# Second routing with per-batch inverses, scaling on the vector engine, normalisation on the scalar engine; feed-forward accumulators in two pairs of banks

## The reference

```python
x = x + 0.5 * ffn(layernorm(x))
x = x + attention(layernorm(x))
x = x + 0.5 * ffn(layernorm(x))
```

```python
att = softmax(where(causal, (q @ k.T) / sqrt(16), -1e10))
y = (att @ v).reshape(B, T, C) @ Wp.T + bp
```

## Time and profile before

| | us |
|---|---|
| median of 3 runs | 2720.24 |
| profiled execution, own time | 2707.74 |
| its span | 2706.0 |
| first feed-forward, about | 146 to 575 |
| attention, about | 575 to 2012 |
| second routing | 2012 to 2276 |
| second feed-forward | 2276 to 2706 |

### The profile page before, as it was taken

One profiled execution on the slowest core, in us unless ns is written; L12 is line 12 of the kernel. 1 busy time (PEld: TensorE's weight loads), 2 busy tenths in 40 slices (PEclk: granted clock), 3 DMA queues, 4 the chain that ended last, 5 costly groups with the idle time before them and its releaser, 6 DMA issues. The chain is left out here.

```text
span 2706.0 us, 43185 instructions
## 1 busy us (share of the span) xinstructions
PE 2227.9 (82%) x14740; PEld 1451.9 (54%) x14740; DVE 1699.0 (63%) x5181; ACT 1218.6 (45%) x2442; POOL 966.9 (36%) x1344
## 2 busy tenths in 40 slices
PE   6659999935699999999999999999962664899997
PEld 6658888834334444444444444443322664788886
DVE  7435555433477877877878878877733663555552
ACT  1224444411056665665666665666750212344443
POOL 3723434326423333333333333330002564333442
PEclk9999999965589999999999999999986775999999
DMA  9552223021524434435344344344315424323220
GB/s 341 187 197 96 88 71 104 29 73 58 132 64 110 117 84 111 112 86 130 87 110 114 86 97 111 80 105 99 80 60 124 144 69 165 126 71 100 77 71 22
DMA packets 185131, 283.21 MB, mean 105 GB/s; under 512 B 14392, under 2 KB 147704, under 8 KB 176720
## 3 DMA queue, kind: packets, MB, share of 16 engines
q1 hardware_dynamic: 170576, 247.08, 34.0%
q0 software_dynamic: 14336, 33.38, 3.5%
HBM read 153.99 MB, written 126.88 MB: 104 GB/s over the span
## 5 line engine op out<-in xcount | busy, mean ns | idle before, releaser
L1646 ACT ACTIVATE at_probs<-at_score_ps 128x512 f32<-128x512 f32 (+3 forms) x1536 | 692.9, 497 | 451.6 <-PE at_score_ps L1763 312.6
L1525 DVE CUSTOM_DVE_ANT_0 at_junk<-at_max_ps,at_causal 128x128 f32<-128x128 f32 (+3 forms) x1024 | 485.5, 484 | 128.2 <-PE at_max_ps L1749 126.2
L1749 PE MATMUL at_max_ps<-at_k,at_q 96*128 96x512 bf16 (+3 forms) x1536 | 494.1, 341 | 43.1 <-DVE at_peak L1525 30.7
L1760 PE MATMUL at_score_ps<-at_q,at_k 99*128 99x512 bf16 (+3 forms) x1536 | 499.3, 332 | 10.7 <-DMA at_v<-v_rows 4.4
L1528 DVE TENSOR_REDUCE at_peak<-at_max_ps 128x1 f32<-128x512 f32 x512 | 352.4, 688 | 118.2 <-PE at_max_ps L1749 114.9
L1037 DVE TENSOR_TENSOR f_hid_lo<-f_hid,f_hid_hi 128x512 fp32r<-128x512 f32 x256 | 177.5, 693 | 322.8 <-ACT f_hid_hi L1061 322.2
L1749 PEld LDWEIGHTS at_max_ps<-at_k,at_q 96*128 96x128 bf16 x1536 | 144.6, 98 | 398.0 <-DVE at_peak L1525 192.0
L1058 ACT ACTIVATE f_hid<-f_hid_ps 128x512 f32<-128x512 f32 x256 | 153.3, 599 | 413.7 <-PE f_hid_ps L1084 413.5
L1773 PE MATMUL at_o_ps<-at_probs,at_v 128*32 128x512 f32 (+3 forms) x3072 | 337.8, 512 | 1.2 <-ACT at_probs L1646 0.7
L1099 PE MATMUL f_y_ps<-f_w_hi,f_hid_hi 128*128 128x256 f32 x1024 | 292.7, 286 | 47.4 <-DVE f_xe L1015 28.9
L1099 PE MATMUL f_y_ps<-f_w_hi,f_hid_lo 128*128 128x256 f32 x1024 | 291.4, 285 | 0.0
(11 more groups left out here) (175 smaller groups left out, 3631.0 us busy)
## 6 DMA issues: line engine op xcount, KB each, us to landing
f_w_raw<-in_w SPq DMA_DIRECT2D x32, 1024.0 KB, 7.6
qk<-at_parts SPq DMA_DIRECT2D x32, 768.0 KB, 4.2
expert_in<-r_zeros SPq DMA_DIRECT2D x16, 1040.0 KB, 11.3
f_xe<-expert_in SPq DMA_DIRECT2D x32, 520.0 KB, 7.3
v_rows<-at_v_outs SPq DMA_DIRECT2D x32, 512.0 KB, 6.2
at_v<-v_rows SPq DMA_DIRECT2D x32, 512.0 KB, 10.4
o_rows<-at_o_out SPq DMA_DIRECT2D x64, 256.0 KB, 2.0
at_q<-qk SPq DMA_DIRECT2D x32, 384.0 KB, 7.6
```

The source lines that it names most:

```text
L1525: v.tensor_tensor_reduce(junk[bank(k, r)][:, 0:w], src, causal[:, HALF - w:HALF], 1.0, LEAST, ALU.add, ALU.max, out).then_inc(max_used, 1)
L1646: a.activation(probs[t % 2][:, h, c0:c0 + w], score_ps[(GH * t + h) % BANKS][:, 0:w], ACT.Exp, scale=float(SCALE)).then_inc(exp_done, 1)
L1749: te.matmul(max_ps[bank(u, r)][:, 0:w], q[u][0:ROWS, h, i * P:(i + 1) * P], kk[u][0:ROWS, h, k0:k0 + w], start=True, stop=True).then_inc(m ...
L1760: last = te.matmul(out[:, 0:w], kk[u][:, h, j * P:(j + 1) * P], q[u][:, h, hf * HALF + c0:hf * HALF + c0 + w], start=True, stop=not diagonal)
```

## The change

- The inverses of a batch are made in attention, while the next batch is at work: at the second group of batch b+1 SP loads the sums of batch b (128 x 128 values), DVE inverts them in the third group, and SP stores them in the fourth. Only the last batch's are made in the second routing, where they are needed for its own last batch only.
- In the second routing `scale` moves from POOL to DVE, at the head of DVE's loop; `normalize` moves from DVE to ACT, as an Identity with a scale of rstd and a bias of -mean x rstd (`shift`, one more small operation on POOL, one on DVE).
- The loads of outputs and inverses of batch 0 are issued first.
- In the feed-forwards the four accumulators lie by twos in a bank, and there are two such sets, used in turn by blocks; the first down of block b waits for combine(b-2) in place of combine(b-1).

```diff
@@ -486,6 +486,17 @@
+def sums_of(dr, b):
...
+    return (dr["o"].rearrange("(n v) t -> n v t", v=VW)[b * H:(b + 1) * H, D, :]
+            .rearrange("n (e t) -> n e t", t=H * S // P))
...
+def inverses_of(dr, b):
...
+    return dr["inv_sums"][b * H:(b + 1) * H, :].rearrange("n (e t) -> (n e) t", t=H * S // P)
...
 def second_route_block(nc, sh, dr, w):
@@ -513,12 +524,13 @@
         half = [sb(f"half{k}", [P, TPB], F32) for k in range(2)]
+        less_mean = [sb(f"less_mean{k}", [P, TPB], F32) for k in range(2)]
+        shift = [sb(f"shift{k}", [P, TPB], F32) for k in range(2)]
         bits = sb("bits", [P, TPB], I32)
...
         xn = sb("xn", [P, 2, TPQ, C], F32)
-        sums = xn[:].rearrange("p a j c -> p (a j c)")
-        assert TOK * H == P * 2 * TPQ * C
+        sums = sb("sums", [P, H * S // P], F32)
         xt = [sb(f"xt{k}", [P, TPQ, CC, P], F32) for k in range(2)]
@@ -585,34 +597,30 @@
-            sp.dma_start(sums, dr["o"].rearrange("(n v) t -> n v t", v=VW)[:, D, :]).then_inc(sums_loaded, 16)
+            load_o(0)
+            load_inverses(0)
             sp.dma_start(wp[:], dr["wp_t"].rearrange("(c p) o -> p c o", p=P)).then_inc(wp_loaded, 16)
-            load_o(0)
+            sp.dma_start(sums[:], sums_of(dr, B - 1)).then_inc(sums_loaded, 16)
             load_o(1)
+            load_inverses(1)
             sp.wait_ge(sums_inverted, 1)
-            sp.dma_start(dr["inv_sums"], sums).then_inc(sums_stored, 16)
-            sp.wait_ge(sums_stored, 16)
-            load_inverses(0)
-            load_inverses(1)
+            sp.dma_start(inverses_of(dr, B - 1), sums[:]).then_inc(sums_stored, 16)
             for b in range(2, B):
...
                 load_o(b)
+                if b == B - 1:
+                    sp.wait_ge(sums_stored, 16)
                 load_inverses(b)
...
         def _(pool):
-            def scale(b):
-                k = b % 2
-                pool.wait_ge(o_loaded[k], 16 * CC * (b // 2 + 1))
-                pool.wait_ge(inv_loaded, 16 * CC * (b + 1))
-                nc.gpsimd.tensor_tensor(o_in[k][:], o_in[k][:], o_inv[:], ALU.mult).then_inc(y_scaled, 1)
...
             def invert_std(b):
...
                 newton(nc.gpsimd, rstd[k][:].bitcast(F32), half[k][:], tmp[:], newton_step, NEWTON_STEPS * b, sh.passed)
+                nc.gpsimd.tensor_tensor(shift[k][:], less_mean[k][:], rstd[k][:].bitcast(F32), ALU.mult)
                 nc.gpsimd.tensor_copy(sh.x[:, TPB * b:TPB * (b + 1), RSTD], rstd[k][:].bitcast(F32)
@@ -625,15 +633,10 @@
-            scale(0)
-            scale(1)
             invert_std(0)
-            scale(2)
             for b in range(B):
...
                     invert_std(b + 1)
-                if b + 3 < B:
-                    scale(b + 3)
                 if b >= 1:
@@ -722,11 +725,28 @@
+            def normalize(n):
+                b, q = n // QPB, n % QPB
+                if b >= B:
+                    return
+                k = b % 2
+                if q == 0:
+                    act.wait_ge(rstd_ready, b + 1)
+                if n >= 2:
+                    act.wait_ge(xt_ps_ready, n - 1)
+                for a in range(TPQ):
+                    j = TPQ * q + a
+                    last = nc.scalar.activation(xn[:, q % 2, a, :], tile_of(sh.x, TPB * b + j), ACT.Identity,
+                                                bias=shift[k][:, j:j + 1], scale=rstd[k][:, j:j + 1].bitcast(F32))
+                last.then_inc(xn_ready, 1)
...
             act.wait_ge(wp_loaded, 16)
...
                     high(b, h)
+            normalize(0)
+            normalize(1)
             for b in range(B):
@@ -734,6 +754,7 @@
                     nc.scalar.copy(xt[q % 2][:], xt_ps[q % 2][:]).then_inc(xt_ready, 1)
+                    normalize(n + 2)
                     if q == 1 and b >= 1:
@@ -757,6 +778,12 @@
             per_expert = sh.expert_less[:].unsqueeze(1).to_broadcast([P, TPB, E])
...
+            def scale(b):
+                k = b % 2
+                dve.wait_ge(o_loaded[k], 16 * CC * (b // 2 + 1))
+                dve.wait_ge(inv_loaded, 16 * CC * (b + 1))
+                v.tensor_tensor(o_in[k][:], o_in[k][:], o_inv[:], ALU.mult).then_inc(y_scaled, 1)
@@ -779,20 +806,9 @@
                 dve.wait_ge(step, at + 2)
+                v.tensor_scalar(less_mean[k][:], moments[k][:, :, 0], -1.0, None, ALU.mult)
                 rsqrt_seed(v, moments[k][:, :, 1], half[k][:], bits[:], rstd[k][:], step, at + 2).then_inc(stats_ready, 1)
                 v.tensor_copy(sh.x[:, TPB * b:TPB * (b + 1), MEAN], moments[k][:, :, 0])
...
-            def normalize(b, q):
-                k, n = b % 2, QPB * b + q
-                if q == 0:
-                    dve.wait_ge(rstd_ready, b + 1)
-                if n >= 2:
-                    dve.wait_ge(xt_ps_ready, n - 1)
-                for a in range(TPQ):
-                    j = TPQ * q + a
-                    last = v.tensor_scalar(xn[:, q % 2, a, :], tile_of(sh.x, TPB * b + j), moments[k][:, j, 0:1],
-                                           rstd[k][:, j:j + 1].bitcast(F32), ALU.subtract, ALU.mult)
-                last.then_inc(xn_ready, 1)
@@ -834,37 +850,40 @@
                 v.memset(onehot[k][:], 0.0)
-            dve.wait_ge(sums_loaded, 16)
-            v.reciprocal(sums, sums).then_inc(sums_inverted, 1)
+            scale(0)
             dve.wait_ge(wp_hi_ready, 1)
...
                 low(0, h)
+            dve.wait_ge(sums_loaded, 16)
+            v.reciprocal(sums[:], sums[:]).then_inc(sums_inverted, 1)
+            scale(1)
             for b in range(2):
...
                     add(b, q)
+                    if b == 1 and q == 0:
+                        scale(2)
                     if q % 2:
...
             for b in range(B):
-                ahead = b + 2 < B
-                normalize(b, 0)
-                normalize(b, 1)
+                if b + 3 < B:
+                    scale(b + 3)
                 if b >= 1:
                     choose(b - 1)
-                for q in range(2):
-                    normalize(b, 2 + q)
-                    if ahead:
-                        add(b + 2, q)
+                if b + 2 < B:
+                    add(b + 2, 0)
+                    add(b + 2, 1)
                 if b + 3 < B:
...
                     place_rows(b - 1)
-                if ahead:
-                    for q in range(2, QPB):
-                        add(b + 2, q)
-                    if b + 3 < B:
-                        low(b + 3, 1)
+                if b + 2 < B:
+                    add(b + 2, 2)
+                    add(b + 2, 3)
+                if b + 3 < B:
+                    low(b + 3, 1)
+                if b + 2 < B:
                     measure(b + 2)
@@ -906,7 +925,7 @@
         hid_ps = [ps(f"hid_ps{k}", [P, BLK]) for k in range(2)]
-        y_ps = [ps(f"y_ps{k}", [P, C]) for k in range(TPK)]
+        y_ps = [[ps(f"y_ps{k}_{a}", [P, 2, C]) for a in range(TPK // 2)] for k in range(2)]
         xt_ps = [ps(f"xt_ps{k}", [P, BLK]) for k in range(CC)]
@@ -1012,7 +1031,7 @@
                 for t in range(TPK):
-                    last = v.scalar_tensor_tensor(x[:, t, 0:C], y_ps[t][:], x[:, t, COEF:COEF + 1], x[:, t, 0:C],
+                    last = v.scalar_tensor_tensor(x[:, t, 0:C], y_ps[b % 2][t // 2][:, t % 2, :], x[:, t, COEF:COEF + 1], x[:, t, 0:C],
                                                   ALU.mult, ALU.add)
@@ -1090,14 +1109,15 @@
                 pe.wait_ge(hid_lo_ready, FC * b + f + 1)
-                if f == 0 and b >= 1:
-                    pe.wait_ge(y_ready, b)
+                if f == 0 and b >= 2:
+                    pe.wait_ge(y_ready, b - 1)
                 m = f % NHID
...
                     for i, (a, w) in enumerate(((hid_hi, w2_hi), (hid_hi, w2_lo), (hid_lo, w2_hi))):
-                        last = nc.tensor.matmul(y_ps[t][:], a[m][:, rows], w[ws][:, f, :],
-                                                start=(f == 0 and i == 0), stop=(f == FC - 1 and i == 2))
+                        last = nc.tensor.matmul(y_ps[b % 2][t // 2][:, t % 2, :], a[m][:, rows], w[ws][:, f, :],
+                                                start=(f == 0 and i == 0 and t % 2 == 0),
+                                                stop=(f == FC - 1 and i == 2), skip_group_check=True)
                 last.then_inc(hid_free, 1)
@@ -1218,6 +1239,9 @@
         o_stored = [sem(f"o_stored{k}") for k in range(2)]
+        sums_loaded = sem("sums_loaded")
+        sums_inverted = sem("sums_inverted")
+        sums_stored = sem("sums_stored")
         block = ctx.enter_context(nc.Block())
@@ -1329,6 +1353,15 @@
                 store_o(g, 0)
+                done = g // NG - 1
+                if done >= 0 and g % NG == 1:
+                    for half in range(2):
+                        sp.wait_ge(o_stored[half], 16 * NG * (done + 1))
+                    sp.wait_ge(sums_stored, 16 * done)
```

(8 more changed lines are left out.)

## The result

The median is now 2643.49 us (2637.23 to 2645.89, 4 runs) beside 2719.99 for the kernel before (now 4 runs): a ratio of 0.9717, 95% interval 0.9699 to 0.9736, or 76.5 us less. The profiled execution took 2642.3 us, span 2640.5, which is 65.4 less than the profiled one of before (2707.74). The two differences are told apart by the blocks, read from where SP issues the first load of each.

What follows compares the result with a forecast made beforehand. PE was taken to bound feed-forwards and attention, a closed chain through POOL's queue the second routing (transfers after the change). -35.1 + 3 - 35.8 = -68 us, from the median 2720.2 to 2652 us, range 2634 to 2674.

Steps and rivals of the forecast that it cites:

- Feed-forwards, -35.1: Both feed-forwards: the block-start stall of 1.17 us goes in full, 15 x 2 times, 35.1 us less.
- rival (2): Feed-forwards: the stall only moves, to the low part or the shared bank; 10 of 35 us left, 2677; chance 0.06.
- rival (4): Feed-forwards: PE without its pauses loses its granted clock, slower than before, 2800 in its example; chance 0.03.
- Attention, +3: Attention: seven reciprocals on DVE ahead of the ring of maxima cost 3 us, the middle between 0 and 6.
- the upper bound: Attention: all DVE time of the seven reciprocals is passed on, 7 x 0.85 = 6 us.
- Start, 13 us earlier: Second routing, start: the first scale begins at 2031.4, 13 us before its row of 2044.5.
- Loop, bound by transfers at 17.8 us a batch: Second routing, loop: two pairs of loads a batch, 8.9 us each, take more time than any engine.
- The sum of the routing, -35.8: Second routing: its end comes at 2232.9 in place of 2268.7, 35.8 us less.
- The rule on 8 and 16 engines: Second routing loads: 8 heads in the slowest dimension limit them to 8 transfer engines; otherwise gain some 14 us larger.
- (1): Second routing: DVE's scales and lows hold up POOL, 4.7 us a turn; 20 us of gain gone, 2672; chance 0.13.
- (3): Second routing: transfers are not the bound, as loads of two kinds overlap better; 2638; chance 0.08.
- The sum on the median: Whole kernel: -68 us taken from the median of the runs, 2720.2, giving 2652 us.

Runs made afterwards that it cites:

- e1: The kernel before with only the feed-forward part of the change (two accumulator sets, wait for the combine two blocks back): 2682.15 us, ratio 0.9874.
- e2: The changed kernel with the old wait for the previous block's combine put back, accumulators still by twos in a bank: 2673.57 us, ratio 0.9843.
- e8: The changed kernel with five reciprocals in place of one at each of the seven places in attention: 2677.12 us, ratio 0.9854.
- e9: The changed kernel with scale back on POOL and normalisation back on DVE, leaving only the early start in the routing: 2670.79 us, ratio 0.9822.
- e4: The changed kernel with loads of outputs and inverses laid out with 16 rows outermost in place of 8 heads: 2631.33 us, ratio 0.9682.
- e3: The changed kernel with high put ahead of the normalisation on ACT in the second routing: 2627.05 us, ratio 0.9672.
- e7: The changed kernel with scale back on POOL, normalisation still on ACT: 2660.52 us, ratio 0.979.

## Why the prediction was right, and where it wasn't

- **Feed-forwards, -35.1.** Right in mechanism and size: 18.0 and 18.4 in the profiles, 35.7 in e1; pitch 23.50 as derived from the slices. PE idle alone (29.0) would have been too little; the pitch was the right measure. Sharing a bank costs 0 (e2), and PE keeps its clock, 1.00 in the second feed-forward: no rival (2), no rival (4).
- **Attention, +3.** One reciprocal measured 0.95 us, not 0.82, and costs nothing to be seen: attention was 1422.5 to 1431.8 us in the ten kernels with one, 1430.0 and 1435.5 in the two without. The middle between two bounds was taken where the slack of the ring was to be asked for; and the upper bound was none, as e8 shows: of each 4.9 us some 2.6 were covered, and what stuck out cost more than its own length.
- **Start, 13 us earlier.** The first scale is 15.6 us after the block's start, for 19.2 forecast and 32.3 before: the step holds, 3.6 too long since outputs and inverses together load faster than each alone. The block as a whole gained 9.1 us by the early start alone (e9).
- **Loop, bound by transfers at 17.8 us a batch: wrong.** This step failed. Its 8.9 us for a pair came from bytes over time in a stretch that the closed chain over POOL set. So it was what the chain asked for and not what the queues can give. At 205 GB/s a pair takes 1.05 / 0.205 = 5.1 us, 10.2 a batch, and e4 shows the late turns untouched by the rate. In place of it stood a chain that the forecast didn't look for. It costed ACT by its busy time ("no limit") and did not name what is queued on ACT behind the new wait for rstd, which was `high`. e3 shows this chain and its price, 15.3 us.
- **The sum of the routing, -35.8 for 39.3, is partly luck.** First to last scale took 119.2 us for a forecast of 130.6 (early turns 12 to 18 us as loads are faster, late ones 21.6); last scale to the end of the last scatter took 82.3 for 70.9, since scatters lagged in the late turns and waited for places: those behind the last scale began 16.0 us after it, at 2155.3, for 8.9 forecast. The two errors of 11.4 cancel, and the 3.6 of the start is what is left.
- **The rule on 8 and 16 engines.** The trace agrees with what the Trainium skill ("DMA: Bandwidth & Descriptors", Why a DMA increments its semaphore by 16 and not by 1) says: with 16 rows outermost the share of engines went from a half to all. But it did not speak against this change as I had it, since the rate rose by a seventh only and was no limit of the late turns.
- **Rivals.** (1) A DVE operation with two SBUF inputs does hold POOL: the scatter beside a scale took 2.25 for 0.97, and none outside the last weight split did with scale on POOL (e7). But it is 1.3 us a turn, not 4.7: the lows and adds cost 0.1. (3) Was right that transfers are not the bound, and wrong that the turn would be POOL's.
- **Against which time.** The sum on the median (2652 for 2643.5) had the right base. By the profiled execution alone (2640 for 2642.3) it looks better than it was: that execution had a first routing 14 us short.

## What to carry to other kernels

When a wait is moved to another engine, write down what that engine has queued behind it and whether the old work needs the wait; a late operand put ahead of independent work closes a chain however idle the engine is, and turning round two lines undid it here, for 15 us. A rate read from a stretch that another chain sets is demand, not capacity: read it where the queue is never empty. For cheap work put on an engine beside the full one, ask how far the full one is ahead: up to that the work is free, past that it cost more than its own length here.

## What the runs showed of the hardware

- Pauses of PE of up to 3.7 us, one in each batch of attention, went with a mean granted clock of 0.96 for 0.99 of 2.4 GHz: 17.8 us more busy time for the same matmuls in 972 us, beside 10.6 us of idle time (e8). About half of the slices with a lowered clock lie at the pauses.
- Loads of outputs (4 KB runs, 8 heads outermost) ran at 131 GB/s, inverses at 125, both in flight together at about 205, each time with half of the transfer engines busy. With 16 rows outermost all engines were busy at about 235. Why the engines carry less each is open; no run tells it.
- An Identity of 128x256 on ACT with scale and bias from SBUF takes about 0.55 us (1.09 for two), inside the 0.2 to 0.6 assumed.
- The first routing, the same in all fourteen programs, took 146 us in one profile and 158 to 161 us in the other thirteen. From 40 to 80 us PE was busy for 37.9 us in the one and for 28.8 to 29.8 in the others, at a granted clock of 1.00 in all; the cause is open.
